# A graph network on one core: 23 of 49 target blocks of the edge layer read their source rows by gather instead of from a sorted grid

## The chip, the cores and the metric

The kernel runs on one core of one Trainium2 chip. The metric is the device time of one execution in microseconds (us).

## What is computed

Four graph layers over one graph of 6250 nodes with 64 features and 206250 edges sorted by target; after each, x is replaced by layernorm(x + layer(x)). The last one, on which most of the change bears, works on edges:

```
L0: h = relu(sum over edges of x[src] @ W_rel + b + x @ W_root), twice
L1: h_q = leaky(h @ Qw.T + Qb); weighted mean of h_q[src] by target; dense; leaky; norm, twice
L2: h1 = x + spmm(x); h2 = spmm(x * x); h1 @ W1.T + b1 + h2 @ W2.T + b2
L3: x_i, x_j = x[src], x[dst]
    h = relu(concat(x_i, x_j - x_i) @ W1 + b1)
    messages = relu(h @ W2 + b2)
    out = segment_sum(messages, dst) / max(degree(dst), 1)
```

## The kernel before

Nodes lie in 49 blocks (BLOCKS) of 128 (P). The kernel has no index reads in its inner loops: it first builds, for each pair of blocks, the 128 x 128 matrix of edge counts (a_d in DRAM) and of edge weights (w_d), and the layers L0 to L2 are products of a block's features with such matrices. A value in float32 that goes through bf16 matmuls is cut into three bf16 parts that sum to it (X3 = 192 columns a node).

The stages in order, with their times in the profiled execution:
- the build of the matrices, to about 1125 us;
- CONV1 and CONV2 (L0), to 2016. In CONV2 POOL fetches the edge lists (gpsimd_dense, two indirect DMAs a chunk, L1755) and DVE shapes them into records (tile_records, L2055): 14 chunks (RCH) of 128 tiles of 128 edges. A target block has TPB = 36 tiles. PE turns the three fields of a chunk (turn_records, L2349) and ACT lays them in recs: source block + 1 or so, source row + 1, target row + 1;
- MEAN1 and MEAN2 (L1), to 3010. Each goes through 13 quads of target blocks (QUADS), the last with one block. A quad's step on PE is seven pieces of w_d (PIECES; L2441, float32) that SP loads into a ring of four (W_SLOTS, L1709). Beside it runs the **sort**: of each target block, the edges are put into 50 tiles (BUCKETS), one for each source block and one for the node's own loop, so that a tile has edges from one source block alone. On DVE a sort is mark (L2098, L2100) and rank_slots (L2107 to L2123), on PE sum_base (L2365), 36 matmuls of place (L2373) and turn_grid (L2380), and ACT copies between them. SP stores the result (store_grid, L1699) as grid_d: for each tile the source rows and the target rows of its 128 slots. Two sorts go with each step: blocks 2n and 2n + 1 with step n. After the quads that complete seven blocks (PART_OF) DVE and PE finish that part of the nodes: part_norms, part_turn, part_q (MEAN1 only), part_dense, part_table;
- BY_SRC (L2), to 3261: 13 quads from at_d, loaded in pieces into a ring of 11 (L1724), while the first grids of the edge stage come in behind them;
- the edge stage (L3), 3282 to 4431. Groups of up to 8 tiles (GT), 7 a block, the seventh with 2 tiles: 343 groups.

What a group of the edge stage does: SP copies its slot rows from grid_d to all partitions (L1740, a ring of 12, ROWS_AHEAD); DVE compares them with the partition's number (mark_rows, L2229), which gives one-hot matrices in bf16 for source and target; PE multiplies the target block's table and, for each tile, the source block's table, which is in SBUF (x3(5)), with them (first_layer, L2508 and L2515); ACT takes the relu (L1880); PE does the second layer (L2526, L2529); ACT and DVE cut the messages into three bf16 parts (L1887, L2245, L1894, L2253); DVE makes the one-hot matrix that sends each slot to its target (mark_targets, L2236); PE adds the messages (L2542). PE's order is first_layer(n), second_layer(n-1), add_messages(n-3). DVE's is rests, mark_rows(n+2), lowest_parts, mark_targets. POOL has no work in this stage.

All queues are in program order, with semaphores between engines; nothing plans their order at run time. A flag that DVE computes in the build (bad, L663) sends the kernel down a general path with per-edge gathers if a block has over TPB * P edges, if a pair of blocks has over 128, or if the lists are otherwise unusual. With the inputs here the fullest target block has 4401 edges and the fullest pair 246 with the loops still in it, and the profiled execution goes the dense way. What is shown below is the dense way.

Of the kernel before, what the change touches and what calls it, by code (L numbers as in the profile page):

```python
# [11 lines left out]
P = 128  # L12
# [20 lines left out]
LAYERS = 6  # L33
# [37 lines left out]
EG = -(-BUCKETS // GT)  # L71
EGROUPS = BLOCKS * EG
# [34 lines left out]
def build(nc, x_in, src_in, dst_in, w_in, edges_in, halves_in, firsts_in, coarse_in, mats_in, rows_in, qb_in, e2b_in, out):  # L107
    from contextlib import ExitStack
    ctx = ExitStack()
    with ctx:  # L110
# [21 lines left out]
        grid_d = dram("grid_d", [BLOCKS, BUCKETS, 2, P], BF16)  # L132

# [159 lines left out]
        d_loop = kept[:, 14 * P:15 * P]  # L293
        slot_low = kept[:, :].bitcast(BF16).rearrange("p (b n two) -> p b n two", n=BUCKETS, two=2)
# [4 lines left out]
        rec_fields = words(REC_FIELDS_AT, 6 * P).rearrange("p (a k e) -> p a k e", a=2, k=3)  # L299
# [19 lines left out]

        ring_b = halfwords(0, ROWS_AHEAD * GT * 2 * P).rearrange("p (a t f n) -> p a t f n", a=ROWS_AHEAD, f=2, n=P)  # L320
# [86 lines left out]
        with scope:  # L407
# [11 lines left out]
            pairs_made, hot_fields = sem("pairs_made"), sem("hot_fields")  # L419
            marked, base_summed, base_kept = sem("marked"), sem("base_summed"), sem("base_kept")  # L420
# [87 lines left out]
        def vector_build(dve):  # L508
# [150 lines left out]
            step(v.tensor_scalar(bad[both, 1:2], bad[both, 1:2], float(TPB * P), None, ALU.is_gt))  # L659
# [988 lines left out]
        def group_tiles(g):  # L1648
            return min(GT, BUCKETS - g * GT)

        def part_over(m):

            k, at = divmod(m + 1, EG * PER_BANK)
            return k - 1 if m >= 0 and at == 0 else None

        def group_tile(g, j, half):

            return g * GT + j + half * (group_tiles(g) // 2)

        def sync_dense(sp):  # L1660
# [18 lines left out]

            for n in range(STREAMS):  # L1680
                load(n)
# [5 lines left out]
            for n in range(STREAMS, 2 * BLOCKS):  # L1687
                load(n)
                if STREAMS <= n < STREAMS + BLOCKS:
                    store_turned(n - STREAMS)  # L1690
            for j in range(2):
# [3 lines left out]
            def store_grid(i):  # L1695
                sp.wait_ge(grid_laid, i + 1)
                for f in range(2):
                    with nc.allow_non_contiguous_dma(reason="slot rows of one target block"):
                        sp.dma_start(grid_d[i, :, f, :], grid_t[f * BUCKETS:(f + 1) * BUCKETS, i % 2, :])\  # L1699
                            .then_inc(grid_stored[i % 2], 16)  # L1700

            for n in range(2 * QUADS):
                g = n % QUADS
                cols = quad_blocks(g) * P
                for j in range(PIECES):
# [5 lines left out]
                    if j in (2, 6):  # L1711
                        block = 2 * n - 3 + j // 6
                        if 0 <= block < BLOCKS:
                            store_grid(block)
            sp.wait_ge(w_used, 2 * QUADS * PIECES)
            for i in range(QUADS * PIECES):
# [3 lines left out]
                elif i == 0:  # L1720
                    sp.wait_ge(placed, BLOCKS)
# [4 lines left out]
            for j in range(2):  # L1726
                sp.wait_ge(grid_stored[j], 32 * -(-(BLOCKS - j) // 2))
# [6 lines left out]

            for m in range(EGROUPS):
                b, g = divmod(m, EG)
# [915 lines left out]
```

## Time and profile before

| | us |
|---|---|
| median of 3 runs | 4412.54 |
| lowest, highest | 4408.51, 4425.93 |
| the profiled execution | 4432.76 |
| its span, first to last instruction | 4430.9 |
| busy PE, PE weight load, DVE, ACT, POOL | 3692.9, 2680.7, 3162.4, 1654.5, 190.2 |
| mean granted TensorE clock, share of full | 0.895 |

The profile shows one execution. PE is TensorE, DVE VectorE, ACT ScalarE, POOL GpSimd, SP SyncE, PEld the load of weights into TensorE; L2441 is line 2441 of the kernel. A row of a timeline has start, duration, engine, line, operation, the written and read tensors, the shape, how often it is repeated there, and in brackets the idle time before it with what ended it. Durations of pipelined instructions overlap with the next by some 0.06 us, so the distance of two starts is the better price. The tensor "arena" holds most buffers of all stages, "tab" the tables, "acc" is PSUM.

### The profile page before, as it was taken

The numbers are of one execution on the slowest core, as the hardware profiler recorded it, in microseconds if no ns is written. First come the engines' busy times: TensorE is split into PE (matmuls) and PEld (weight loads), VectorE is DVE, ScalarE is ACT, GpSimd is POOL, SyncE is SP. The second block draws the span as 40 slices with busy tenths as digits, with TensorE's granted clock in tenths as the row PEclk, the third lists the DMA queues.
The fourth block names the chain that finished last, engine by engine and source line by source line (L and its number), as shares of the span: only waits on it lengthen the run. The fifth ranks groups of instructions, "written<-read, shape, count | busy, mean of one in ns | idle before, by whom it ended". The sixth has DMA issues, their size and how long they took to land.

```text
span 4430.9 us, 114162 instructions
## 1 busy us (share of the span) xinstructions
PE 3692.9 (83%) x50334; PEld 2680.7 (60%) x50335; DVE 3162.4 (71%) x4651; ACT 1654.5 (37%) x3728; POOL 190.2 (4%) x187
## 2 busy tenths in 40 slices
PE   0766667666888888889989698988989999999999
PEld 0555555555666668784443343437977777777776
DVE  2877777774667674338999899993457777777777
ACT  0666666663556652001010000000014444444444
POOL 6111110100000000000000000000000000000000
PEclk7777877876899999999999799898989999999999
DMA  2788888886689988668888498778954444444442
GB/s 48 244 261 259 260 260 267 257 254 228 207 266 290 286 272 316 263 233 378 340 325 356 152 373 339 281 294 305 349 184 146 141 146 146 142 142 149 142 141 84
DMA packets 533795, 1055.49 MB, mean 238 GB/s; under 512 B 36624, under 2 KB 440656, under 8 KB 492848
## 3 DMA queue, kind: packets, MB, share of 16 engines
q1 hardware_dynamic: 525104, 1031.11, 66.5%
q0 software_dynamic: 8192, 16.99, 1.6%
q8 instruction: 403, 6.60, 0.6%
q14 instruction: 96, 0.79, 0.1%
HBM read 730.46 MB, written 317.56 MB: 237 GB/s over the span
## 4 chain that ended last, share of the span: by engine, by line
PE 52%; DVE 22%; ACT 13%; issue 10%; DMA 2%; POOL 1%; DVEq 0%; ACTq 0%; SPq 0%; POOLq 0%
PE acc L2400 8%; PE acc L2529 6%; ACT arena L1787 6%; PE acc L2508 5%; PE acc L2515 4%; PE acc L2483 4%; PE acc L2542 4%; PE acc L741 3%; PE acc L745 3%; DVE arena L2123 2%; ACT a_line L690 2%; PE acc L2441 2%; ACT w_line L690 2%; PE acc L2526 2%; PE acc L833 2%
## 5 line engine op out<-in xcount | busy, mean ns | idle before, releaser
L2441 PE MATMUL acc<-arena,tab 128*64 128x512 f32 (+1 forms) x2548 | 642.5, 599 | 3.7 <-DMA arena<-w_d 2.2
L745 PE MATMUL acc<-hot_c,hot_s 64*128 64x50 bf16 x12544 | 469.1, 201 | 156.4 <-issue 156.1
L690 ACT CAST a_line<-acc 128x392 bf16<-128x392 f32 x784 | 441.5, 565 | 370.0 <-PE acc L745 363.0
L741 PE MATMUL acc<-hot_c,hot_s 64*128 64x100 bf16 x6272 | 462.5, 227 | 127.6 <-issue 75.8
L745 PEld LDWEIGHTS acc<-hot_c,hot_s 64*128 64x128 bf16 x12544 | 425.8, 109 | 166.5 <-issue 166.0
L741 PEld LDWEIGHTS acc<-hot_c,hot_s 64*128 64x128 bf16 x6272 | 347.4, 102 | 242.0 <-issue 161.6
L690 ACT COPY w_line<-acc 128x392 f32<-128x392 f32 x784 | 450.3, 577 | 0.0
L2400 PE MATMUL acc<-tab,arena 128*128 128x192 bf16 x4802 | 440.9, 255 | 6.3 <-DVE r L1952 3.4
L2245 DVE SCALAR_TENSOR_TENSOR arena<-acc,arena 128x512 f32<-128x512 f32 (+1 forms) x343 | 217.5, 634 | 301.1 <-ACT arena L1887 294.7
L2400 PEld LDWEIGHTS acc<-tab,arena 128*128 128x128 bf16 x4802 | 419.2, 102 | 17.3 <-issue 5.6
L1787 ACT CAST arena<-acc 128x512 bf16<-128x512 f32 (+1 forms) x637 | 326.4, 562 | 219.1 <-PE acc L2419 216.4
L2441 PEld LDWEIGHTS acc<-arena,tab 128*64 128x64 f32 x2548 | 197.9, 143 | 329.8 <-issue 312.3
L2529 PE MATMUL acc<-w_pair,arena 128*128 128x128 f32 x2450 | 370.0, 292 | 0.0
L2529 PEld LDWEIGHTS acc<-w_pair,arena 128*128 128x128 f32 x2450 | 304.0, 193 | 71.2 <-issue 67.9
L2027 DVE TENSOR_REDUCE deg_b<-arena 128x49 f32<-128x6272 bf16 x49 | 327.3, 6679 | 0.9
L2419 PE MATMUL acc<-ident_b,arena 128*128 128x128 bf16 x2401 | 244.0, 227 | 89.1 <-ACT arena L1787 66.6
L1880 ACT ACTIVATE arena<-acc 128x512 f32<-128x512 f32 (+1 forms) x343 | 189.0, 551 | 339.1 <-PE acc L2515 338.3
L2542 PE MATMUL acc<-arena 128*128 128x192 bf16 x2450 | 264.4, 250 | 23.5 <-DVE arena L2253 23.5
L1887 ACT ACTIVATE arena<-acc 128x512 bf16<-128x512 f32 (+1 forms) x343 | 189.0, 551 | 254.0 <-PE acc L2529 253.8
L2515 PEld LDWEIGHTS acc<-arena,tab 128*64 128x64 bf16 x7350 | 244.7, 111 | 61.6 <-issue 2.4
L596 DVE TENSOR_TENSOR hot_c<-hot_c,parts_w 128x2400 bf16<-128x2400 bf16 x196 | 274.5, 1401 | 0.0
L2508 PE MATMUL acc<-arena 128*64 128x512 bf16 (+1 forms) x2058 | 268.6, 369 | 6.9 <-DVE arena L2229 6.9
(267 smaller groups left out, 5536.0 us busy)
## 6 DMA issues: line engine op xcount, KB each, us to landing
arena<-w_d SPq DMA_DIRECT2D x168, 1792.0 KB, 9.2
w_d<-w_line SPq DMA_DIRECT2D x49, 3136.0 KB, 17.4
arena<-a_d SPq DMA_DIRECT2D x98, 1568.0 KB, 8.1
arena<-grid_d SPq DMA_DIRECT2D x294, 512.0 KB, 3.6
a_d<-a_line SPq DMA_DIRECT2D x49, 1568.0 KB, 5.9
at_d<-arena SPq DMA_DIRECT2D x49, 1536.0 KB, 11.0
arena<-at_d SPq DMA_DIRECT2D x84, 896.0 KB, 6.6
arena<-w_d SPq DMA_DIRECT2D x14, 448.0 KB, 3.5
```

Source lines behind the costliest of these rows:

```text
L596: v.tensor_tensor(products.rearrange("p (a k) n -> p a k n", k=3), ones_of.unsqueeze(2).to_broadcast([P, OCT, 3, CW]), parts.unsqueeze(2). ...
L690: ins = nc.scalar.copy(to[:, :, :, i * WG:(i + 1) * WG], of[:, :, m, 0:BLOCKS, :])
L741: mm(to[h], hot_s[rows_of, o, j, :], hot_c[rows_of, o, j:OCT + 3 * j + 1:OCT + 2 * j, :], start=k == 0, stop=True, skip_group_check=True)
L745: last = mm(to[h][:, CW:], hot_s[rows_of, o, j, :], hot_c[rows_of, o, OCT + 3 * j + part, :], start=False, stop=True, skip_group_check=True)
L1787: nc.scalar.copy(at_line[b % 2][:, t * QUAD * P:t * QUAD * P + cols], bank(2 + m % 2)[:, 0:cols]).then_inc(at_laid, 1)
L2027: node(v.tensor_reduce(deg_b[:, :], counts_of(n % STREAMS).rearrange("p (b d) -> p b d", d=P), AX.X, ALU.add))
L2400: last = mm(bank(6 + n % 2)[:, 0:X3], line[:, s * P:(s + 1) * P], table[:, s, :], start=s == 0, stop=s == BLOCKS - 1)
L2441: last = mm(bank(6 + n % 2)[half, 0:cols], table[:, s * D:(s + 1) * D], w_pieces[:, i % W_SLOTS, d * QUAD * P:d * QUAD * P + cols], start= ...
L2508: mm(z[h][:, 0:side * P], tgt3[:, b, part * D:(part + 1) * D], rows_of[:, h * side:(h + 1) * side, 1, :], start=part == 0, stop=False, ski ...
L2515: last = mm(z[h][:, j * P:(j + 1) * P], x3(5)[:, tile if tile < BLOCKS else b, part * D:(part + 1) * D], rows_of[:, h * side + j, 0, :], s ...
L2529: last = mm(bank(2 + m % 2)[:, j * P:(j + 1) * P], h_e[:, m % 2, j * P:(j + 1) * P], w2_pair[:, :], start=False, stop=True, skip_group_che ...
L2542: last = mm(bank(4 + b % 2)[:, 0:X3], tgt_hot[:, m % HOT_SETS, h * side + j, :], msg_e[:, m % MSG_SETS, 2 * j + h, :, :].rearrange("p k f ...
```

## The change

23 target blocks (3, 5, ..., 47; GATHERED) are no longer sorted. Their edges stay in the order of the records: 36 tiles in 5 groups, of which 35 (REAL) can hold edges. For them
- DVE computes in MEAN2 the node number of each edge's source (fetch_rows, six operations of 128 x 828), the own-loop records decoded to the block's own rows;
- SP stores, in CONV2, the target rows of each chunk (tgt_rows_d, 14 stores of 128 rows of 256 bytes), and the record fields become bf16, with one more operation in tile_records, so that records of a neighbouring block get target 0;
- when the edge table is complete, SP stores it to DRAM (table3_d, 6272 rows of 384 bytes, 2.4 MB), after four groups' rows instead of twelve, and then goes on with the rows;
- POOL then gathers each tile's 128 source rows by an indirect DMA into fetched3, a ring of 6 groups (FETCH_SETS), 23 x 35 = 805 DMAs; a set is free when the group six fetched groups back has its first layer (edge_sums);
- in first_layer PE takes a gathered tile as the stationary operand and the identity as the moving one, which turns it, in place of the source table and a one-hot matrix; a group waits for all its gathers first;
- mark_rows has only the target half to do for such a group.

The other 26 blocks are sorted one a step: block SORTED[n] with step n of MEAN1 and MEAN2, the last one in the last step. The grid of that one is turned by PE after the last dense products of MEAN2, laid by ACT and stored by SP before SP begins the loads of BY_SRC. The edge stage has 297 groups of 2128 tiles in place of 343 of 2450. The flag's limit goes from 36 to 35 tiles, 4480 edges.

```diff
+GATHERED = range(3, BLOCKS, 2)
+SORTED = [b for b in range(BLOCKS) if b not in GATHERED]
+REAL = TPB - 1
...
-            step(v.tensor_scalar(bad[both, 1:2], bad[both, 1:2], float(TPB * P), None, ALU.is_gt))
+            step(v.tensor_scalar(bad[both, 1:2], bad[both, 1:2], float(REAL * P), None, ALU.is_gt))
...
+            def store_target_rows(c):
+                sp.wait_ge(recs_shaped, c + 1)
+                with nc.allow_non_contiguous_dma(reason="one row a tile"):
+                    sp.dma_start(tgt_rows_d[c * P:(c + 1) * P, :], rec_fields[:, c % 2, 2, :])\
+                        .then_inc(rows_kept[c % 2], 16)
...
-                    if j in (2, 6):
-                        block = 2 * n - 3 + j // 6
-                        if 0 <= block < BLOCKS:
-                            store_grid(block)
+                    if j == 6 and n >= 1:
+                        store_grid(n - 1)
+            store_grid(len(SORTED) - 1)
             sp.wait_ge(w_used, 2 * QUADS * PIECES)
...
+            for m in range(4):
+                load_rows(m)
+            sp.wait_ge(dense_out, CHUNKS * LAYERS)
+            sp.dma_start(table3_d.rearrange("(b p) f -> p b f", p=P), x3(5)).then_inc(table3_stored, 16)
+            for m in range(4, EGROUPS):
+                load_rows(m)
...
+            pool.wait_ge(fetch_known, 1)
+            pool.wait_ge(table3_stored, 16)
+            for a, m in enumerate(FETCHED_GROUPS):
+                b, t, _ = EDGE_GROUPS[m]
+                if a >= FETCH_SETS:
+                    pool.wait_ge(edge_sums, FETCHED_GROUPS[a - FETCH_SETS] + 1)
+                for u in range(real_tiles(m)):
+                    at = GATHERED.index(b), t + u
+                    pool.indirect_dma_start(
+                        fetched3[:, a % FETCH_SETS, u, :], None, table3_d,
+                        bass.IndirectOffsetOnAxis(fetch_idx[:, at[0], at[1]:at[1] + 1], 0)
+                    ).then_inc(row_fetched[a % FETCH_SETS], 16)
...
-                v.tensor_scalar(to[:, 2, :], d_low, 1.0, None, ALU.add)
+                v.tensor_scalar(d_next, d_low, 1.0, None, ALU.add)
                 node(v.scalar_tensor_tensor(d_loop, d_low, float(OWN_FROM), d_loop, ALU.is_ge, ALU.mult))
+                v.scalar_tensor_tensor(to[:, 2, :], d_wrong, 0.0, d_next, ALU.is_equal, ALU.mult)
...
-                    if 2 * n + 1 < BLOCKS:
-                        mark(2 * n + 1)
                     if k is not None:
                         part_q(p, k)
-                    if 2 * n < BLOCKS:
-                        rank_slots(2 * n)
+                    rank_slots(n)
                     if k is not None:
                         part_table(p, k)
-                    if 2 * n + 2 < BLOCKS:
-                        mark(2 * n + 2)
-                    if 2 * n + 1 < BLOCKS:
-                        rank_slots(2 * n + 1)
+                    if n + 1 < len(SORTED):
+                        mark(n + 1)
+                    if p == MEAN2 and g == 1:
+                        fetch_rows()
...
-                        if j == PIECES - 1 and 2 * n < BLOCKS:
-                            place(2 * n)
+                        if j == PIECES - 1:
+                            place(n)
...
+            turn_grid(len(SORTED) - 1)
             pe.wait_ge(dense_out, CHUNKS * LAYER[BY_SRC])
-            pe.wait_ge(grid_laid, BLOCKS)
+            pe.wait_ge(grid_laid, len(SORTED))
...
+                if b in GATHERED:
+                    a = fetch_slot(m)
+                    before_it = sum(real_tiles(FETCHED_GROUPS[i]) for i in range(a % FETCH_SETS, a + 1, FETCH_SETS))
+                    pe.wait_ge(row_fetched[a % FETCH_SETS], 16 * before_it)
...
+                            elif u < real_tiles(m):
+                                last = mm(to, fetched3[:, a % FETCH_SETS, u, of], ident_b[:, :], start=False,
+                                          stop=part == 2, skip_group_check=True)
```

## Rows read from the trace of the kernel before

**Rows 1.** Busy time by stage: stretch, its length, busy of each engine, PEclk, DMA share, GB/s.

```profile
2016.00:3010.00 994.00, 874.55 (x5215) 402.11 (x5217) 913.67 (x986) 94.03 (x328) 0.00 (x0) 0.92 0.79 311
...
3282.00:4431.00 1149.00, 1116.58 (x14651) 851.88 (x14651) 842.20 (x1491) 535.14 (x1036) 0.00 (x0) 0.98 0.41 138
```

**Rows 2.** Timeline of DVE in MEAN1: the starts of two sorts in a row.

```profile
2382.54 1.08 DVE L2098 TENSOR_TENSOR arena<-iota_c,arena 128x1800 bf16<-128x1800 bf16 x1
...
2398.75 1.08 DVE L2098 TENSOR_TENSOR arena<-iota_c,arena 128x1800 bf16<-128x1800 bf16 x1
```

**Rows 3.** Timeline of ACT: the copy of a quad's sums, once a step.

```profile
2044.01 0.60 ACT L1868 COPY tab<-acc 128x512 f32<-128x512 f32 x1
...
2384.14 0.60 ACT L1868 COPY tab<-acc 128x512 f32<-128x512 f32 x1
2416.96 0.60 ACT L1868 COPY tab<-acc 128x512 f32<-128x512 f32 x1
2459.71 0.60 ACT L1868 COPY tab<-acc 128x512 f32<-128x512 f32 x1
...
2556.17 0.60 ACT L1868 COPY tab<-acc 128x512 f32<-128x512 f32 x1
...
3002.03 0.60 ACT L1868 COPY tab<-acc 128x512 f32<-128x512 f32 x1
```

**Rows 4.** Timeline of PE in MEAN1 and MEAN2.

```profile
2398.37 1.80 PE L2373 MATMUL acc<-arena 128*128 128x100 bf16 x36 [2.71 <-DVE arena L2123]
...
2407.71 6.23 PE L2441 MATMUL acc<-arena,tab 128*64 128x512 f32 x28
...
2524.16 6.57 PE L2441 MATMUL acc<-arena,tab 128*64 128x512 f32 x14 [0.72 <-DVE r L1952]
...
2698.04 0.43 PE L871 MATMUL acc<-bi_stack,xT 128*128 128x64 f32 x2
...
2704.80 5.00 PE L2441 MATMUL acc<-arena,tab 128*64 128x512 f32 x14
```

**Rows 5.** Busy time of 20 us of MEAN1, columns as in rows 1.

```profile
2056.00:2076.00 20.00, 19.66 (x139) 8.20 (x139) 19.66 (x14) 2.04 (x8) 0.00 (x0) 1.00 1.01 428
```

**Rows 6.** One line's instructions: min/median/max ns, first and last start.

```profile
L2508 PE MATMUL acc<-arena x2058: 219/379/637, 3282.5 to 4416.4; 128*64 128x512 bf16 x161, 128*64 128x128 bf16 x27
```

**Rows 7.** Timeline of PE in CONV2: the turn of one chunk of records.

```profile
1749.46 0.94 PE L2354 MATMUL acc<-ident,arena 128*128 128x128 f32 x6 [2.01 <-DVE arena L2075]
```

**Rows 8.** Timelines of SP and PE between MEAN2 and BY_SRC.

```profile
3011.00 38.83 SPq L1724 DMA_DIRECT2D arena<-at_d  x15
...
3038.23 11.99 PE L2483 MATMUL acc<-tab,arena 128*128 128x192 bf16 x121 [2.79 <-DVE r L1949]
```

**Rows 9.** Timelines of POOL and DVE in the build: indirect DMAs, and what DVE runs.

```profile
66.69 0.94 POOL L486 DMA_INDIRECT fine<-firsts_in,coarse_i  x1 [0.30 <-issue]
67.94 0.94 POOL L486 DMA_INDIRECT fine<-firsts_in,coarse_i  x1 [0.30 <-issue]
...
108.44 3.30 POOL L503 DMA_INDIRECT fetch<-halves_in,row_of  x1 [0.30 <-issue]
109.53 1.40 DVE L596 TENSOR_TENSOR hot_c<-hot_c,parts_w 128x2400 bf16<-128x2400 bf16 x1
...
191.81 1.40 DVE L596 TENSOR_TENSOR hot_c<-hot_c,parts_w 128x2400 bf16<-128x2400 bf16 x1
192.59 1.45 POOL L503 DMA_INDIRECT fetch<-halves_in,row_of  x1 [30.33 <-PE acc L709]
```

**Rows 10.** Groups by line, whole span: busy us, mean ns; idle before and its releaser.

```profile
L2229 DVE TENSOR_SCALAR arena<-arena,part_iota 128x2048 bf16<-128x2048 bf16 (+1 forms) x343 | 235.5, 687 | 0.0
...
L2236 DVE TENSOR_TENSOR arena<-iota_b,kept 128x1024 bf16<-128x1024 bf16 (+1 forms) x343 | 215.1, 627 | 0.0
L2253 DVE TENSOR_TENSOR arena<-arena 128x512 bf16<-128x512 f32 (+1 forms) x343 | 215.0, 627 | 0.0
```

**Rows 11.** DMA issues of the page: KB each, median us to landing.

```profile
at_d<-arena SPq DMA_DIRECT2D x49, 1536.0 KB, 11.0
```

More of the change, by code:

```diff
@@ L70 @@
 GT = 8
-EG = -(-BUCKETS // GT)
-EGROUPS = BLOCKS * EG
+GATHERED = range(3, BLOCKS, 2)
+SORTED = [b for b in range(BLOCKS) if b not in GATHERED]
+REAL = TPB - 1
+EDGE_GROUPS = [(b, t, min(GT, tiles - t)) for b in range(BLOCKS)
+               for tiles in (TPB if b in GATHERED else BUCKETS,) for t in range(0, tiles, GT)]
+EGROUPS = len(EDGE_GROUPS)
+LAST_GROUP = [max(m for m in range(EGROUPS) if EDGE_GROUPS[m][0] == b) for b in range(BLOCKS)]
+FETCHED_GROUPS = [m for m in range(EGROUPS) if EDGE_GROUPS[m][0] in GATHERED]
+FETCH_SETS = 6
 ROWS_AHEAD, HOT_SETS, MSG_SETS = 12, 4, 4
@@ L1646, in quad_blocks, with gathered_of, group_tiles, block_over @@
             return min(QUAD, BLOCKS - g * QUAD)
-        def group_tiles(g):
-            return min(GT, BUCKETS - g * GT)
-        def part_over(m):
[L1653 to L1658, printed above, removed]
+        def gathered_of(k):
+            first, last = GATHERED[0] * TPB, (GATHERED[-1] + 1) * TPB
+            return recs[:, k, first:last + TPB].rearrange("p (b k) -> p b k", k=2 * TPB)[:, :, 0:TPB]
+        def group_tiles(m):
+            return EDGE_GROUPS[m][2]
+        def block_over(m):
+            return EDGE_GROUPS[m][0] if 0 <= m < EGROUPS and m == LAST_GROUP[EDGE_GROUPS[m][0]] else None
+        def part_over(m):
+            b = block_over(m)
+            return b // PER_BANK if b is not None and b % PER_BANK == PER_BANK - 1 else None
+        def fetch_slot(m):
+            return FETCHED_GROUPS.index(m)
+        def real_tiles(m):
+            return min(EDGE_GROUPS[m][2], REAL - EDGE_GROUPS[m][1])
         def sync_dense(sp):
@@ L1690, in sync_dense @@
                     store_turned(n - STREAMS)
+                at = n - BLOCKS - STREAMS - 6
+                if at >= 0 and at % 3 == 0:
+                    store_target_rows(at // 3)
+            for c in range((BLOCKS - STREAMS - 7) // 3 + 1, RCH):
+                store_target_rows(c)
             for j in range(2):
@@ L2304, in vector_dense @@
                     mark_targets(n - 1)
-                if n >= 4 and (n - 3) % EG == 0 and (n - 4) // EG < BLOCKS:
-                    take_edges((n - 4) // EG)
+                if block_over(n - 4) is not None:
+                    take_edges(block_over(n - 4))
                 if part_over(n - 4) is not None:
```

172 lines of the change are left out of this document (96 added, 76 removed).

## The prediction

> **What bounds the kernel now.** I read the busy times by stage first, to find the stages that the change touches: the two weighted passes (2016 to 3010 us: PE busy 875 and DVE 914 of 994 us, moving 311 GB/s) and the edge stage (3282 to 4431: PE busy 1117 of 1149 us, POOL 0) [rows 1]. Then, inside them, the timelines, where a step of the loop is the distance between two copies of its sums.
>
> In the weighted passes DVE sets most steps. One sort takes it 2398.75 - 2382.54 = 16.2 us, of which 0.5 is the copy of a quad's sums, so 15.7 [rows 2]. Two sorts are 31.4, and a plain step in MEAN1 lasts 32.8, one that also finishes a part of seven blocks 42.8 (2384.1 to 2417.0 to 2459.7). The eleven full steps of MEAN1 after the first, six with a part, take 2459.7 - 2044.0 = 415.7 us, those of MEAN2 3002.0 - 2556.2 = 445.9; with plain steps near 30 that makes a part step of MEAN2 49.3 [rows 3]. PE is close behind: it waits for the last operation of a rank (L2123), 2.7 us in the step shown [rows 4]. And where the steps are densest the DMA share is 1.01, at 428 GB/s [rows 5]: that is the wall of this stage, since each full step loads 7 pieces of 1.835 MB, 12.85 MB, hence 30.0 us.
>
> In the edge stage PE is the bound: its first-layer matmuls start from 3282.5 to 4416.4, so a block of 50 tiles takes 1134/49 = 23.1 us [rows 6]. POOL does nothing there now; after the change it has 805 gathers to issue.
>
> **The change, part by part.**
>
> Sorting, 49 blocks to 26. A step keeps one sort. PE: pieces that follow each other start 3.1 us apart (28 records in 6.23), a piece followed by something else costs about 0.5 more, its last matmuls' tail; with four of the latter 7 x 3.1 + 4 x 0.5 = 23.7, plus one placement 1.8 and about 1.5 of small turns and base sums: 27 to 27.5 for a plain step [rows 4]. A ring of four pieces lets the DMA run ahead in part steps, so only the mean of two steps must stay over 30.0. MEAN1, part step: the part adds what it adds now, 42.8 - 32.8 = 10 us, less about 1 that then lies under the loads' slack; the rank still stands behind the query products on DVE: 36.5. Eleven steps are 6 x 36.5 + 5 x 27.5 = 356.5, so -59. The end of MEAN1 (its last step has one block, so PE has little to do while DVE still does two sorts) lasts 2524.2 - 2459.7 = 64.5 us [rows 3, 4]; with one rank and one mark (16 us) in place of almost three sorts (41) it is 39: -25. MEAN2, part step: DVE has 31.4 of sorts and 18 of norms and table; less 15.7 it has 34, and PE becomes the later one: 27.5 + 6.8 of dense products (2698.04 to 2704.80) + some 3 of turns and 2 of wait for the norms = 39.5 [rows 4]. Eleven steps are 374.5, so -71. The short last step of MEAN2 has no sort now and gets one, in front of the last norms on DVE: +9. With a first step or two unchanged, the sum is -146; I take -140, for the loads' wall. Bounds: 314.7 MB at 0.428 are 735 us plus about 45 us in which nothing can be loaded (the ends and the start), which allows at most -210; if each step keeps the plain 30 us and parts gain half, -70.
>
> Records (CONV2). The three turns take bf16 where they took float32: 0.94 us now [rows 7], some 0.35 then, 14 times: -8. PE waits there for DVE's last operation, and DVE gets one more of about 0.3 us: +4. Net -5 (bounds -13 and +4). SP stores 14 times 32 KB of target rows behind loads that wait for a later block sum: nothing.
>
> The order on SP before BY_SRC. Now the last grid is stored in the last full step, and SP loads 11 pieces from 3011.0 while PE waits for the last norms; PE starts at 3038.2 [rows 8]. After the change the store of the last grid waits for a turn that PE does behind the last dense products, and the loads are queued behind that store: the 27 us of lead are gone. PE then waits for the first piece, some 5 us; after that a piece of 0.92 MB needs 2.1 us at 428 GB/s against 18/7 = 2.6 on PE. +4 (bounds 0 and +15).
>
> The edge stage, PE alone. A gathered block has 36 tiles in 5 groups for 50 in 7; a tile's products are the same shapes. 14/50 of 23.1 is 6.5; with the fixed share of a group I take 6.3, so 16.8. 23 blocks: -145; the stage would be 1004 us. DVE falls too (row marks half as wide, fewer tiles) and stays free.
>
> The edge stage, POOL. 23 x 35 = 805 gathers of 128 rows, one after the other. The trace shows such a gather at 0.94 us and the next 1.25 us after the start of the last with DVE idle (rows of 256 B; the one of 768 B below, its hold taken off, is as long) [rows 9]. A pair of one sorted and one gathered block needs 35 x 1.25 = 43.8 us of POOL, and PE 23.1 + 16.8 = 39.9: **POOL is the bound even at its best**, and only the six sets ahead hide its first ones. It isn't at its best: a gather that starts under a DVE operation with two SBUF inputs is held until that operation ends. The one at 192.59 took 1.45: the operation from 191.81 ends at 193.21, and 0.83 later, at 194.04, so does the gather, which is a gather without its first 0.1 us; the one at 108.44 was held through two of them (3.30) [rows 9]. In the edge stage the lowest parts (L2253) and the target marks (L2236) are such operations, some 0.63 us apiece for 7 tiles on average (215 us for 343 of either), near 13 us in a pair of 86 tiles less the overlap of their ends, over some 48 us: a chance of 0.27, times half of 0.6, is 0.08 a gather, 0.16 if both in a row hold it. The row marks (L2229, one SBUF input, 236 us for 2450 tiles; a gathered tile is half as wide: 50 + 18 tiles, 6 us a pair) [rows 10] never met a gather in the trace: 0 to 0.14, and I take 0.05 as the nearer to the reads that were not held. That is 1.38 us a gather (bounds 1.25 and 1.55). The Trainium skill ("SBUF — State Buffer", Who interferes with whom) says that a tensor_scalar in a two-port mode shuts GpSimd out for the whole instruction. By it the row marks would cost the upper 0.14 rather than 0.05.
>
> POOL can't start before the table is stored: SP waits for the last dense output, then stores 2.4 MB; a store of 1.5 MB landed in 11.0 us [rows 11], with a free queue I take 12 (8 to 18). After the last gather come its landing (4), the last group (2), a sorted block (23) and the tail from the last first layer to the end, 4431 - 4416 = 15. Edge stage = 12 + 44 + 805c = 56 + 805c: 1167 us at c = 1.38, +18.
>
> **Sum.** -140 - 5 + 4 + 18 = -123 us. The profiled execution takes 4432.8 (span 4430.9), so 4310; the median of the runs is 4412.5, 20 below it, and the same difference gives **4290 us**. In general the change is 805c - 1234 us: even at c = 1.53.
>
> **The rivals.**
>
> Free gathers. Holds don't matter since DVE idles while PE waits for rows, so c = 1.25: edge 1062, total -228, 4185 us. For it: POOL is then late and DVE has gaps (some 28 us busy of 44). Against it: the held gathers in the trace at a busy DVE. 0.17.
>
> The weighted passes give only half (-70): the loads, already at 428 GB/s for 60 us on end, and their waits keep the steps. Total -53, 4359 us. 0.16.
>
> Slower: POOL gets through only where DVE does none of its two-input operations and row marks. They are 12.9 + 5.7 = 18.6 us a pair, of which four fifths fall on a gather: 43.8 + 15 = 58.6 us a pair, c = 1.67, against 46.2 now for two sorted blocks. Edge 1400, total +110, 4523 us. It decides from c = 1.53. For it: the gather of 3.30 us. Against it: most of those under such operations were held only by the one they started in. 0.16. The rule of the Trainium skill named above ("SBUF — State Buffer", Who interferes with whom) speaks for the row marks' share of it.
>
> That the gathered path isn't taken at all (a block over 4480 edges sends the kernel the general way) is out: the inputs' fullest block has 4401.
>
> My forecast, POOL-bound near 1.38 with most of the sorting gain: 0.51. The range, 4170 to 4470, takes in free gathers, the half gain and c up to 1.5 and ends before the slower case. 0.5% (22 us) is about what a measurement of this kernel can tell from no change. Faster 0.77, within 0.08, slower 0.15.
>
> **What would show it.** Weighted passes near 855 us with DVE busy near 550 and a step's idle time of PE ended by the norms, not by L2123; DMA share over 0.85. POOL in the edge stage without a gap, 805 gathers near 1.08 us each; PE waiting in gathered blocks for a landing, sorted blocks still 23 us, PE's granted clock under 0.98. A start of the first gather some 12 us after the last dense output. I am wrong if POOL waits for edge sums (PE is the bound), if a gather takes under 1.0 or over 1.25 us on average, or if the steps of the weighted passes stay at 32 us or more.

## The result, and the profile after

| us | before | after |
|---|---|---|
| median (runs) | 4417.84 (4) | 4223.38 (4) |
| lowest, highest | 4408.51, 4425.93 | 4209.69, 4230.16 |
| the profiled execution, its span | 4432.76, 4430.9 | 4230.16, 4228.3 |
| CONV1 and CONV2 | 890.7 | 884.3 |
| the two weighted passes, first to last product with w_d | 994.2 | 827.0 |
| from there to the first product of BY_SRC | 27.5 | 36.9 |
| BY_SRC | 244.3 | 244.8 |
| the edge stage, first first-layer product to the end | 1148.4 | 1114.5 |

The ratio is 0.9557, 95% interval 0.952 to 0.959: 194 us or 4.4% faster. The stages are cut at the first and last starts of their matmuls. What is left, the build, took 1125.8 and 1120.8; in the runs below it is 1100 to 1125 whatever the kernel, so spans are compared stage by stage. Here 158 us came from the weighted passes with their end, 34 from the edge stage and 6 from CONV1 and CONV2. A stage of the same code varies from profile to profile as well: in the kernels below the weighted passes with one sort a step take 824 to 831 us, the stretch behind them mostly 36.6 to 39.4, CONV1 and CONV2 881 to 888, the edge stage with 805 gathers 1113 to 1116.

Busy time by stage after, columns as in [rows 1]: the weighted passes, the edge stage.

```profile
2005.10:2832.10 827.00, 779.25 (x4292) 346.95 (x4293) 560.57 (x734) 69.33 (x211) 0.00 (x0) 0.96 0.91 373
3113.80:4228.30 1114.50, 1002.75 (x12650) 764.04 (x12650) 713.51 (x1306) 465.17 (x898) 813.57 (x805) 0.94 0.51 140
```

In the weighted passes DVE's busy time fell from 914 to 561 us, PE's share rose from 0.88 to 0.94 and the DMA share from 0.79 to 0.91. In the edge stage PE is busy 1003 of 1114 us, where it was 1117 of 1149, at a granted clock of 0.94 for 0.98.

The copies of a quad's sums on ACT, the rulers of the steps as in [rows 3]: the first step's, the last full one of MEAN1, the first and last full ones of MEAN2.

```profile
2032.69 0.61 ACT L1925 COPY tab<-acc 128x512 f32<-128x512 f32 x1
...
2390.35 0.59 ACT L1925 COPY tab<-acc 128x512 f32<-128x512 f32 x1
...
2458.84 0.61 ACT L1925 COPY tab<-acc 128x512 f32<-128x512 f32 x1
...
2822.95 0.61 ACT L1925 COPY tab<-acc 128x512 f32<-128x512 f32 x1
```

Eleven steps of MEAN1 take 357.7 us (415.7 before), its end 68.5 (96.5), eleven of MEAN2 364.1 (445.9). A plain step is 26 to 28 us (the first of each pass 30), a part step 36 to 38.7.

What PE waited for in the weighted passes (us in total, times, longest), and then what DVE waited for most:

```profile
PE acc L2510 <- DMA arena<-w_d: 16.0, 26, 1.4
PE acc L850 <- DVEq L2066: 14.9, 7, 6.4
PE acc L2442 <- DVE arena L2196: 8.2, 4, 4.8
```

```profile
DVE sums_d L2077 <- PE acc L2455: 107.7, 23, 10.5
```

L2196 is the last operation of a rank; PE waited 54.0 us for it before and 8.2 now. L850 is a turn that waits for the norms. DVE now waits for PE's sums instead. Loads were late 26 times, by 16 us in all (4 times and 2 us before).

In the edge stage, the longest waits of POOL and of PE, and the gathers (one line's instructions) with their count, least, median and greatest duration in ns and their first and last start:

```profile
POOL tab L1818 <- PE acc L2594: 4.8, 5, 3.6
```

```profile
PE acc L2594 <- DMA tab<-table_d,qT: 81.1, 30, 5.7
```

```profile
L1818 POOL DMA_INDIRECT tab<-table_d,qT x805: 940/947/1450, 3124.9 to 4186.0; - x161
```

POOL is the bound: between its first gather and its last it waited for PE 7 us in all, and for nobody else, and PE waited 81 us for rows. 1061.1 us for 804 distances is 1.320 us a gather. The first starts 11.1 us after the stage begins, and 42.3 us follow the start of the last.

### The profile page after: what moved, and what is told of

Read it like the earlier page. It is cut to its first block and busy times, and to the rows that moved or that the text cites. A ratio compares the mean times of both kernels' runs of the same rounds, so it can differ in the third digit from the quotient of the medians.

```text
span 4228.3 us, 107905 instructions
## 1 busy us (share of the span) xinstructions
PE 3469.7 (82%) x47394; PEld 2519.8 (60%) x47395; DVE 2690.1 (64%) x4234; ACT 1560.5 (37%) x3476; POOL 1000.9 (24%) x992
## 5 line engine op out<-in xcount | busy, mean ns | idle before, releaser
L1818 POOL DMA_INDIRECT tab<-table_d,qT x805 | 813.6, 1011 | 1441.4 <-DMA table_d<-tab 1193.0
L2510 PE MATMUL acc<-arena,tab 128*64 128x512 f32 (+1 forms) x2548 | 616.5, 592 | 17.6 <-DMA arena<-w_d 16.0
L762 PEld LDWEIGHTS acc<-hot_c,hot_s 64*128 64x128 bf16 x12544 | 419.4, 108 | 165.6 <-issue 165.5
L758 PEld LDWEIGHTS acc<-hot_c,hot_s 64*128 64x128 bf16 x6272 | 343.6, 101 | 244.9 <-issue 162.1
L2315 DVE SCALAR_TENSOR_TENSOR arena<-acc,arena 128x512 f32<-128x512 f32 (+2 forms) x297 | 188.9, 636 | 393.7 <-ACT arena L1945 390.2
L2606 PE MATMUL acc<-w_pair,arena 128*128 128x128 f32 x2128 | 332.5, 299 | 0.0
L2606 PEld LDWEIGHTS acc<-w_pair,arena 128*128 128x128 f32 x2128 | 274.2, 200 | 64.5 <-issue 60.0
L1938 ACT ACTIVATE arena<-acc 128x512 f32<-128x512 f32 (+2 forms) x297 | 164.1, 553 | 393.0 <-PE acc L2594 199.7
L520 POOL DMA_INDIRECT fetch<-halves_in,row_of x100 | 111.6, 1116 | 707.4 <-PE acc L726 670.1
L1805 POOL DMA_INDIRECT kept<-edges_in,d_row_of x28 | 26.4, 945 | 1011.6 <-DVE d_row_of L2110 801.7
L2488 PEld LDWEIGHTS acc<-ident_b,arena 128*128 128x128 bf16 x2401 | 144.6, 99 | 184.8 <-ACT arena L1850 184.8
```

Of the source, the lines that this page charges most:

```text
L758: mm(to[h], hot_s[rows_of, o, j, :], hot_c[rows_of, o, j:OCT + 3 * j + 1:OCT + 2 * j, :], start=k == 0, stop=True, skip_group_check=True)
L762: last = mm(to[h][:, CW:], hot_s[rows_of, o, j, :], hot_c[rows_of, o, OCT + 3 * j + part, :], start=False, stop=True, skip_group_check=True)
L1818: pool.indirect_dma_start(fetched3[:, a % FETCH_SETS, u, :], None, table3_d, bass.IndirectOffsetOnAxis(fetch_idx[:, at[0], at[1]:at[1] + 1 ...
L2315: v.scalar_tensor_tensor(rest_e[:, m % 2, 0:nt * D].rearrange("p (t f) -> p t f", t=nt), bank(2 + m % 2)[:, 0:nt * D].rearrange("p (t f) - ...
L2488: turn = mm(bank(2 + m % 2)[:, u * P:(u + 1) * P], line[:, s * P:(s + 1) * P], ident_b[:, :], start=True, stop=True)
L2510: last = mm(bank(6 + n % 2)[half, 0:cols], table[:, s * D:(s + 1) * D], w_pieces[:, i % W_SLOTS, d * QUAD * P:d * QUAD * P + cols], start= ...
```

## The experiments

Each kernel ran beside the kernel before on the same chip. sort_alone, edge_alone, early_grid and the two kernels with 21 gathered blocks ran four or five times; the other six ran once, so of them the stages of their one profile are read. Where a kernel leaves work out, its results are not the layer's, and only its time is used.

### One half at a time

**sort_alone.** 26 blocks are sorted, nothing is gathered, and every block goes through the sorted path.

```diff
-                for tiles in (TPB if b in GATHERED else BUCKETS,) for t in range(0, tiles, GT)]
+                for tiles in (BUCKETS,) for t in range(0, tiles, GT)]
-            sp.dma_start(table3_d.rearrange("(b p) f -> p b f", p=P), x3(5)).then_inc(table3_stored, 16)
-            for a, m in enumerate(FETCHED_GROUPS):
...
```

> The sorting half of the change alone: 26 sorts, one a step, as in the changed kernel, and an edge stage with 49 blocks of 50 tiles as before (a block that isn't sorted reads the grid and the low numbers of the sorted block in front of it, so its sums are not the right ones); no gathers, no table store, no target rows stored. My theory (a step lost one sort of 15.7 us on DVE and is now bound by PE and the loads): weighted passes 827 us and 37 us behind them as in the changed kernel, 158 us less than before, edge stage 1149 as before, total -160 to -165 us, about 4255. Rival (the sorting gain comes in part from less of something else that the gathers changed): total under -130 or over -190.

Measured: ratio 0.960 (0.957 to 0.964), 4244.5 us. The weighted passes 827.5 and 36.9, as in the kernel after; the edge stage 1148.4, as before to the tenth. The whole is 176 us shorter than the kernel before where 160 to 165 were expected; the profile puts the excess in the stages ahead (the build 1105.0 us for 1125.8, CONV1 and CONV2 880.7 for 890.7), not in what the experiment is about.

**edge_alone.** All 49 blocks are sorted on the old schedule, and the 23 are then gathered all the same.

```diff
-SORTED = [b for b in range(BLOCKS) if b not in GATHERED]
+SORTED = list(range(BLOCKS))
+SORTS_IN = [2] * 24 + [1, 0]
...
```

> The edge half alone: all 49 blocks are sorted, two a step as before, and 23 of them are then gathered by POOL in the edge stage all the same. My theory (the edge stage is set by 805 gathers at 1.32 us, 12 us ahead of them and 42 behind): edge stage 1115 us, weighted passes 994 as before, total -35 to -42 us, about 4378. Rival (the edge stage gained from what the sorting left behind, or costs elsewhere what it saves): total between -15 and +20.

Measured: ratio 0.9905 (0.987 to 0.994), 4372.9 us. Weighted passes 1001.9 and 25.2 (5 us more than before together; no run tells why), edge stage 1113.1. So by stages the two halves add up (the product of their ratios is 0.951 for 0.956, since the build varies), and the edge half alone gains 35 us in its stage, where I had forecast a loss of 18: 805 gathers from 3269.5 to 4329.8 are 1.319 us each.

### Is POOL the bound of the edge stage

**half_gathers.** Every second gather is left out, and PE reads the tile before.

```diff
-                for u in range(real_tiles(m)):
+                for u in range(0, real_tiles(m), 2):
...
```

> The changed kernel with every second gather left out: an odd tile's matmuls read the rows of the even tile in front of it (so its sums are not the right ones), 414 gathers instead of 805, all matmuls kept. My theory (POOL sets the edge stage): it falls to PE's own time, 1149 - 23 x 6.3 = 1004 us, PE doesn't wait for gathers, its granted clock is back at 0.98, total 4120. Rival (PE is the bound already, its work slower by the granted clock of 0.94 or by what the turned tiles cost): the stage stays over 1080 us.

Measured: 4098.9 us in one run, edge stage 998.9. What POOL waited for in it, and the busy time of its edge stage:

```profile
POOL tab L1818 <- PE acc L2594: 373.0, 22, 34.1
```

```profile
3098.00:4097.00 999.00, 966.19 (x12650) 742.22 (x12650) 712.52 (x1307) 464.87 (x898) 427.13 (x414) 0.98 0.47 137
```

POOL now waits for PE, 373 us of it, and PE's own time comes out: 999 us, against 1004 in the prediction (23.1 a sorted and 16.8 a gathered block). The granted clock is back at 0.98.

### What makes a gather cost 1.32 us

**no_target_marks.** The target marks of full groups are left out in the edge stage (the matrices in the buffers are used again).

```diff
+                if m >= HOT_SETS and group_tiles(m % HOT_SETS) == GT:
+                    v.engine_nop().then_inc(tgt_marked, 1)
+                    return
                 v.tensor_tensor(along(tgt_hot[:, m % HOT_SETS, 0:nt, :]), ramp(iota1_b[:, :], nt),
```

> The changed kernel without the target marks of the edge stage (L2306) from the fifth group on: the one-hot matrices of the first four groups stay and are used by all (the sums are not the right ones). Everything else runs. Theory A (an operation with two SBUF inputs holds a gather for the rest of its time, as I costed it): the marks were half of such time, so the cadence of the 805 gathers falls by 0.04, from 1.32 to 1.28 us, edge stage 1114 to 1082. Theory B (in the trace of the changed kernel the gathers whose first 0.1 us fell under such a mark were only 147, and 0.107 us longer on average, 16 us in all): cadence 1.30, edge stage 1098. Rival (the gathers' cadence has nothing to do with these operations): 1.32 and 1114.

**no_row_marks.** The same with mark_rows, from the thirteenth group on.

```diff
+                if m >= ROWS_AHEAD:
+                    v.engine_nop().then_inc(row_marked, 1)
+                    return
                 v.tensor_scalar(of, of, part_iota1[:, :], None, ALU.is_equal).then_inc(row_marked, 1)
```

> The changed kernel without the row marks (L2300) from the thirteenth group on: PE multiplies with the raw numbers that SP loaded (the sums are not the right ones). Theory A (my costing, 0.05 us a gather): cadence 1.27, edge stage 1074. Theory B (by the trace of the changed kernel: 10 us under a gather's start and perhaps 12 where a row mark begins inside a gather): cadence 1.29, edge stage 1092. Rival (with one SBUF input they don't hold a gather at all): 1.32, 1114.

Measured: 4205.0 and 4227.0 us. Distances of 1.311 and 1.327 us, edge stages 1105.5 and 1118.8. The distances that the theories gave (1.27 to 1.30) were missed, by no_row_marks altogether. The four kernels here with the edge stage of the kernel after have distances of 1.319 to 1.323, so both differences are small but outside that spread: taking an operation of 0.5 to 0.7 us out of a group gave 9 us of the stage in one case and lost 4 in the other. Neither is what a fixed price for each hold makes.

**no_holds.** Both, and the lowest parts too.

```diff
...
+                if m >= MSG_SETS:
+                    v.engine_nop().then_inc(msg_ready, 1)
+                    return
                 v.tensor_tensor(msg_e[:, m % MSG_SETS, 0:nt, 2, :],
```

> In the edge stage VectorE does no row marks from the 13th group on, no target marks of full groups and no lowest parts from the fifth group on; the one-hot matrices and lowest parts that are left in the buffers are used again, so the layer's sums are not the reference's. What is left on VectorE there is the rests (L2315, one operand in PSUM), the short target marks of the last groups of a block and a block's sum. Leaving out one kind alone moved the distance of two gathers from 1.320 to 1.311 us (target marks) and to 1.327 (row marks). Theory (VectorE's operations with operands in SBUF delay the gathers, but their delays do not add, since the gathers fall into step with whatever of them is left): with all three gone the distance falls to 1.25 to 1.27 us, the gather's mean duration from 1.01 to about 0.95, and the edge stage from 1114.5 to 1060 to 1075 us. Rival (the extra 0.07 us comes from something else, such as the traffic of the row loads or the wait instructions between gathers): the distance stays at 1.30 or more, the edge stage at 1100 or more.

**targets_twice.** The other direction.

```diff
-                v.tensor_tensor(along(tgt_hot[:, m % HOT_SETS, 0:nt, :]), ramp(iota1_b[:, :], nt),
+                op = (along(tgt_hot[:, m % HOT_SETS, 0:nt, :]), ramp(iota1_b[:, :], nt),
...
+                node(v.tensor_tensor(*op))
+                v.tensor_tensor(*op).then_inc(tgt_marked, 1)
```

> The target marks (L2306) are done twice in each group of the edge stage, the second behind the first; nothing is left out. VectorE gets some 0.55 us more a group, 297 groups. If each operation with two SBUF operands adds its own delay, as my prediction reckoned it, a share of 0.12 more of the time lies under such operations, at half of 0.6 us: +0.035 us a gather, 1.355, the edge stage +28 us to 1142. If the delays do not add because gathers and VectorE's operations fall into step, the distance stays within 0.012 us of 1.320 and the edge stage between 1105 and 1124. Third reading, that a gather pays only for being held by an operation that starts just behind it, at the 0.11 us that the trace shows on average: +0.014, 1.334, the edge stage 1126.

The edge stage of no_holds (windows), its gathers (one line's instructions), and the gathers of targets_twice:

```profile
3097.80:4167.00 1069.20, 990.96 (x12650) 757.31 (x12650) 252.13 (x435) 465.62 (x898) 765.27 (x805) 0.95 0.53 146
```

```profile
L1818 POOL DMA_INDIRECT tab<-table_d,qT x805: 941/947/1276, 3108.2 to 4126.1; - x161
```

```profile
L1818 POOL DMA_INDIRECT tab<-table_d,qT x805: 941/992/1487, 3107.8 to 4208.5; - x161
```

no_holds: 4169.0 us, 1017.9 us for 804 distances are 1.266 (10 us of it POOL's waits for PE), a gather is busy 765.27/805 = 0.951 us, the edge stage 1069.4. That is inside what the theory gave: the three operations with all operands in SBUF make 0.054 of the 0.07 us over 1.25. The rests (L2321 there, one operand in PSUM) run on as before; 144 of the 805 gathers began under one and took 0.947 us on average, the others 0.951: such an operation holds nobody.

targets_twice: 4252.6 us, 1100.7/804 = 1.369, the edge stage 1154.2, 40 us more. The theory that the delays don't add falls for this direction. The simple count said +0.035 a gather, it was +0.049.

What reconciles the runs is where gathers begin. I counted it from the timelines of POOL and DVE between 3130 and 4130 us; "by chance" is the count if starts were spread evenly over the distance of two gathers (ops x time / distance), for the operations of full groups, whose last 0.16 us are left off:

```
kernel, operation       ops   gathers begun in it   by chance   their mean hold   begun 0-0.2 us ahead   by chance
after, target marks     226          42                90           0.27 us              82                  34
after, lowest parts     227          66                90           0.12                 69                  34
after, row marks        138          72                62           0.15                 22                  21
twice, first of two     217          69                84           0.30                 52                  32
twice, second of two    217         112                84           0.14                 53                  32
no_holds, rests         235         107                98           0.003                39                  37
```

Three held gathers in the kernel after (timelines of POOL, then of DVE):

```profile
3186.96 0.99 POOL L1818 DMA_INDIRECT tab<-table_d,qT  x1 [0.30 <-issue]
...
3209.21 1.25 POOL L1818 DMA_INDIRECT tab<-table_d,qT  x1 [0.30 <-issue]
...
3220.88 1.39 POOL L1818 DMA_INDIRECT tab<-table_d,qT  x1 [0.30 <-issue]
```

```profile
3186.45 0.68 DVE L2323 TENSOR_TENSOR arena<-arena 128x512 bf16<-128x512 f32 x1
...
3209.60 0.74 DVE L2300 TENSOR_SCALAR arena<-arena,part_iota 128x2048 bf16<-128x2048 bf16 x1
...
3220.78 0.68 DVE L2306 TENSOR_TENSOR arena<-iota_b,kept 128x1024 bf16<-128x1024 bf16 x1
```

The gather at 3220.88 began 0.10 us into the target marks, which end at 3221.46, and ended at 3222.27, 0.81 later. The one at 3186.96 began in the last 0.17 us of the lowest parts, which end at 3187.13, and ended 0.82 later; it lost 0.04. The one at 3209.21 began under no such operation, but row marks began 0.39 us behind its start, and it ended 0.12 after their end, at 3210.46.

Read over all 805 gathers of the kernel after, two rules give 779 of the durations to within 0.02 us. A gather that begins while target marks, lowest parts or row marks run ends 0.82 us after that operation does, or after its own 0.945 us if that is later. A gather behind whose start row marks begin within 0.5 us ends 0.12 us after their end. A two-input operation that begins behind a gather's start holds nothing: in no_row_marks 226 gathers had none of the three at their start and lowest parts beginning before 0.945 us were over, and took 0.944. So the mean holds of the table are not prices of three kinds of operation; they tell how much of it was left when the gather began (lowest parts 0.12 here, 0.26 in no_row_marks).

Gathers begin somewhere in full target marks and in lowest parts about as often as by chance (119 and 112, 117 by chance), but most of them in the last 0.2 us, where little is left to wait for. The columns "begun 0-0.2 us ahead" count the same meetings for target marks and lowest parts: the operation before is then in its last 0.2 us. What the holds cost, by these rules, as the sum over all gathers of what exceeds 0.945 us, beside what they would cost if the starts were spread evenly (an estimate by the same rules), in us a gather:

```
kernel             measured   starts spread evenly
after                0.066        0.121
no_target_marks      0.053        0.087
no_row_marks         0.070        0.074
targets_twice        0.111        0.151
```

In the kernel after, gathers and DVE's groups have fallen into a step in which nearly half of the cost is missed. Its 52.8 us are 28.0 by row marks (half of it in gathers begun ahead of them), 11.8 by target marks, 9.9 by lowest parts. Without the row marks their 28 us are gone, but so is the step: the gathers begin nearly as if at random, and the holds by the other two grow from 21.7 to 52.2 us. That is why leaving the row marks out gave nothing. What makes gathers and groups lock (that DVE's groups follow PE, and PE waits for rows, is a guess) and at just this distance no run tells.

### The end of MEAN2

**early_grid.** The last grid is turned with the last sums, and SP stores it behind the first eleven loads of BY_SRC.

```diff
-            store_grid(len(SORTED) - 1)
...
+                if i == PIECE_SLOTS:
+                    store_grid(len(SORTED) - 1)
...
+                if p == MEAN2:
+                    turn_grid(len(SORTED) - 1)
```

> The changed kernel with the last grid turned and laid before the last part of MEAN2 and stored by SP behind the first 11 loads of BY_SRC instead of in front of them. My theory (the 5.7 us that PE waits for the first piece come from that order on SP): the 37 us between the last weighted piece and BY_SRC become 31 to 32, total -5 to -6 us against the changed kernel. Rival (the wait is a cold start of the loads, whatever the order): within 2 us.

PE's timeline around the first product of BY_SRC, with the wait ahead of it in brackets, in the kernel after, SP's there, and PE's in early_grid:

```profile
2869.02 16.23 PE L2547 MATMUL acc<-tab,arena 128*128 128x192 bf16 x166 [5.68 <-DMA arena<-at_d]
```

```profile
2863.66 0.65 SPq L1740 DMA_DIRECT2D grid_d<-tab  x2
2864.41 19.04 SPq L1764 DMA_DIRECT2D arena<-at_d  x16
```

```profile
2844.25 15.94 PE L2550 MATMUL acc<-tab,arena 128*128 128x192 bf16 x160 [2.80 <-DVE r L2009]
```

Measured: ratio 0.9553 (0.950 to 0.960). The end went from 36.9 to 32.8 us (36.6 to 39.4 in the other kernels that store the last grid first and rank in full), 4.1 of the 5 to 6 expected, since the norms are then late by 2.8 where the load had been late by 5.7. In the time of a run this can't be seen (4210.7 against 4223.4, ratios 0.9553 and 0.9557).

### Who bounds the weighted passes now

**half_rank.** From the third sort on, four of DVE's operations in a rank are left out.

```diff
-                node(v.tensor_tensor(along(run), along(run), each(base_s[:, i % 2], TPB), ALU.add))
+                if i < 2:
+                    node(v.tensor_tensor(along(run), along(run), each(base_s[:, i % 2], TPB), ALU.add))
...
```

> The first four of VectorE's operations in the rank of a sort (add, multiply, add and reduce, 4.6 us) are left out from the third sort on, so that slots are placed by a rank left over and the edge layer's sums are not the reference's. It tells who bounds the weighted passes of the kernel after the change. Theory (TensorE with its loads bounds the plain steps, the norms' chain the part steps): 24 sorts x 4.6 = 110 us less work on VectorE, but the passes fall only from 827 to 800 to 817 us, nearly all in the part steps and at the ends of the two passes, where the rank stands in front of the last norms; a plain step stays at 27 us. Rival (VectorE still sets the steps, as it did before the change): each step falls by most of the 4.6 us and the passes by 60 us or more, to 765 or less, if the loads at 430 GB/s allow it (735 us + 45).

The weighted passes (windows):

```profile
1989.20:2805.30 816.10, 777.14 (x4292) 341.39 (x4293) 453.67 (x641) 69.27 (x211) 0.00 (x0) 0.96 0.92 378
```

Measured: 4195.4 us. DVE lost 107 us (561 to 454), the passes 11, from 827.0 to 816.1, and the stretch behind them another 6, from 36.9 to 30.7. Plain steps of MEAN1 are 26.1 to 27.6 us, against 26.0 to 27.2. DVE no longer sets the steps. PE and the loads are left, and no run tells them apart: over the eleven steps of MEAN1 in the kernel after PE is busy 0.96 of the time and the DMA share is 0.96 too.

### A better split

Since POOL is the bound at 805 gathers and PE at 414, fewer gathered blocks should even them out. **gathered21** sorts 17 and 33 too, **gathered21_early** has the early grid as well.

```diff
+GATHERED = [b for b in range(3, BLOCKS, 2) if b not in (17, 33)]
+SORTS_IN = [2 if n in (0, 13) else 1 for n in range(2 * QUADS)]
...
```

> The changed kernel with 21 gathered blocks in place of 23 (17 and 33 are sorted too) and 28 sorts; the two more go into the first step of MEAN1 and of MEAN2, their second half into the plain step behind. My theory (edge stage = 12 + 42 + 1.32 a gather until PE's own time is reached): 735 gathers give 1024, PE alone 1149 - 21 x 6.5 = 1012, together about 1030, 85 us less than with 23; the weighted passes within 5 us of 827; total about 4125 to 4140. Rival (with POOL and PE near balance the six sets are too few, and each waits for the other): edge stage over 1060.

> The last kernel with the last grid stored behind the first 11 loads of BY_SRC as well. My theory: both gains add up, 4 us less between the weighted passes and BY_SRC. Rival: PE is the bound of nothing there and the 4 us come back in BY_SRC.

Measured: ratios 0.948 (0.942 to 0.954) and 0.947 (0.943 to 0.951), 4185.4 and 4168.7 us; edge stages 1072.2 and 1067.7, where my count had given 1030, and the rival was right. The weighted passes took 831.0 and 824.1 us; the early grid brought the stretch behind them from 39.3 to 36.0, and BY_SRC stayed at 244.9 us. In the second one's edge stage, POOL's wait and PE's wait:

```profile
POOL tab L1825 <- PE acc L2635: 45.6, 5, 20.6
```

```profile
PE acc L2635 <- DMA tab<-table_d,qT: 36.5, 12, 5.6
```

Both engines wait: where three sorted blocks stand in a row POOL has filled its six sets and sits idle (20.6 and 18.0 us, at the two such places), and in the rest PE waits for it. 53 us + 735 x 1.32 + 45 of POOL's idle time is 1068. A seventh set finds no room in the buffer they lie in. The edge stage is 47 us below the changed kernel's. The two were measured beside different runs of the kernel before (4410.2 and 4417.8 us), so the ratios tell their distance: 0.947 against 0.956, some 40 us, with intervals that don't meet (0.943 to 0.951, 0.952 to 0.959).

## Why the prediction was right, and where it wasn't

The forecast was 4290 us in a range of 4170 to 4470; it is 4223, faster as forecast, and 67 below. By spans it was -123 and is -203: of these 80 us, 5 are the build's scatter, 1 is CONV1 and CONV2, 22 the weighted passes with their end, and 52 the edge stage.

- **The bound of the weighted passes.** Right. MEAN1 -58.0 for -59 (plain 27, part 36 us, for 27.5 and 36.5), its end -28.0 for -25. That a plain step stays at 27 us with less work on DVE is what half_rank shows; whether PE or the loads end it is open.
- **MEAN2's part steps** were mis-sized: 37 to 38.7 us for 39.5, and -81.8 for -71. I had put in 3 us of turns and 2 of waiting for the norms; the trace has 1.8 for a turn (L850) and 1.4 for the norms (8.5 us in six waits), and six times the difference is the 10 us.
- **The loads' wall.** I rounded -146 to -140 for it. PE waited 16 us for loads in the two passes. On average the stage drew 373 GB/s, below the 428 of [rows 5], but MEAN1's eleven steps drew 393 and single ones 426 (from 2126.5 to 2162.7, at a DMA share of 1.00): the wall is near, and was met in places. The rival of half the gain (-70) is out.
- **The short last step and the store ahead of BY_SRC**: +9.9 for +9 and +4. The mechanism on SP is as told, and it costs 4.1 of them by early_grid.
- **CONV2** with CONV1 -6.4 for -5 (the terms given, -8 and +4, add to -4). With 881 to 888 us in the kernels that have this code and one profile before, the trace bears out the sign and not the size.
- **PE's own time in the edge stage**: 999 us for 1004 (half_gathers). **POOL as the bound**: right, with 7 us of waiting for PE; start 11.1 us for 12, tail 42.3 for 44.
- **The step that failed is the price of a gather**, 1.38 us forecast and 1.32 measured, times 805 = 48 us; with it the edge stage was to lose 18 us and gained 34. The base of 1.25 us from the build's rows of 256 B [rows 9] held for rows of 384 B (1.266 with no such operation beside it). That a gather waits for the end of the operation it begins under held too. What failed is "a chance of 0.27": I multiplied a share of DVE's time by half an operation, as if gathers began at random. The two-input operations cost 0.027 us a gather for the 0.08 put in, since most gathers that meet them meet only their ends; with starts spread evenly the rules of the trace would give 0.074 (an estimate), so the sizes put in were sound and the chance was not.
- **The row marks**, 0.05 a gather put in and 0.035 measured in the trace, were right by luck. I took a low value because they might hold less than the others do; they hold as much, and also gathers begun up to 0.5 us ahead of them (0.048 with starts spread evenly, by the same estimate). Nor is that price what leaving them out would save: the distance then rose to 1.327.
- **The rule of the Trainium skill** ("SBUF — State Buffer", Who interferes with whom), by which a tensor_scalar in a two-port mode shuts GpSimd out for the whole instruction, agrees with the trace as far as one gather goes: one begun in row marks ends 0.82 us after their end, and one begun up to 0.5 us ahead of them 0.12 after it. That they ran in such a mode the trace doesn't name. Another rule of the same section, that a DVE operation with at most one SBUF input leaves GpSimd alone outside such modes, is what the rests show in no_holds: 0.947 us for a gather begun under one, 0.951 for the others.
- **The rivals.** Free gathers (4185 us, edge stage 1062) is the floor that no_holds found at 1069; the truth lay between it and my forecast. The slower case, gathers only where DVE is still, is out: a gather begun under the rests costs nothing, and with the marks doubled a gather is at 1.37 us, far from the 1.53 from which the change would lose.

So sign and bounds were right, and the half that I thought a small loss is a small gain: edge_alone has a ratio of 0.9905 with an interval below 1.

## What to carry over

When one engine is loaded so that it becomes the new bound, its price per item is the number that decides, and items that meet another engine's operations need not do so at random: here the two fell into step, and a count by shares of busy time gave up to twice the holds (0.12 us a gather for 0.066), in one kernel the right ones (0.074 for 0.070). Check the term by one run without all such operations, and read in the timelines where the items begin, since leaving out one of three can change the step as well. And cut the work so that the two engines end together, in an order in which the buffer between them is neither full nor empty: two blocks fewer took 47 us off the edge stage, and 39 us of POOL idling at a full buffer are still in it.

## What the runs showed of the hardware

- Gathers of 128 rows from DRAM issued back to back start 1.25 us apart with nothing beside them, 0.94 us of it on POOL and 0.30 between; of 256 B rows in the build and of 384 B rows in the edge stage alike.
- A gather that begins under a DVE operation with all operands in SBUF (target marks, lowest parts, row marks) ends 0.82 us after the end of that operation: the hold is what is left of the operation less 0.13 us, whichever of the three it is. Under one with an operand in PSUM it isn't held: 144 gathers of no_holds took 0.947 us, the others 0.951.
- A two-input operation that begins behind a gather's start doesn't lengthen it (0.944 us over 226 gathers of no_row_marks). Row marks, a tensor_scalar of 2048 columns in 0.74 us, do if they begin within 0.5 us: the gather then ends 0.12 us after them (1.08 us on average for the 84 that began 0.2 to 0.56 us ahead in the kernel after).
- PE's granted clock was 0.98 in the edge stage when it had rows at all times, and lower when it waited for them: 0.96 with 12 such waits (gathered21_early), 0.94 with 30 (the kernel after), 0.93 with 30 longer ones (targets_twice).
